# Decoder kernel on one core: passes written out without barriers, two steps of the attentions reordered, and more idle products on TensorE

## Reference

```
x = x + gated causal self-attention(layernorm(x))      # 16 heads of 16
x = x + rotary cross-attention(layernorm(x), ctx)      # 16 heads
x = x + quantised conv feed-forward(layernorm(x))      # 256 -> 1024 -> 256
x = x + self-attention(layernorm(x))                   # 16 heads, not causal
x = x + one-head cross-attention(layernorm(x), ctx)    # 256 wide
x = x + mixture of experts(layernorm(x))               # top 2 of 16, and a shared one
```

## Time and profile before

| | us |
|---|---|
| median of 3 runs | 3564.23 |
| the profiled execution | 3568.19 |
| its span, first to last instruction (46466 instructions) | 3566.9 |
| start of the four passes (first L1955) | 52.87, 930.92, 1816.92, 2691.84 |
| busy: PE, DVE, ACT, GpSimd | 3231.5 (91%), 2350.4 (66%), 1795.1 (50%), 546.5 (15%) |

### The profile page before, as it was taken

How to read it: one execution, slowest core, us unless ns; L and a number is a source line. 1 busy time by engine, 2 the same in 40 slices (tenths; PEclk the granted TensorE clock), 3 DMA queues, 4 the chain that set the end, 5 groups by cost and what they waited for, 6 DMA issues and landing times. The chain is left out here.

```text
span 3566.9 us, 46466 instructions
## 1 busy us (share of the span) xinstructions
PE 3231.5 (91%) x17428; PEld 1735.4 (49%) x17428; DVE 2350.4 (66%) x4375; ACT 1795.1 (50%) x2562; POOL 546.5 (15%) x990
## 2 busy tenths in 40 slices
PE   5998889999899878999999988899998998799999
PEld 3544432368644433236864444323786444432477
DVE  5864578746585557865668556785666744788566
ACT  2454636653346454665344545466434454546643
POOL 0111010014111101002411110100240111010033
PEclk8898979999989897999998989899999898889999
DMA  3222011113021201201302120110231201011023
GB/s 130 39 38 40 1 28 28 19 49 115 30 46 34 37 1 28 37 10 58 112 25 55 25 37 1 36 28 22 68 101 38 39 16 37 1 36 37 23 69 101
DMA packets 119358, 149.14 MB, mean 42 GB/s; under 512 B 25445, under 2 KB 77159, under 8 KB 118835
## 3 DMA queue, kind: packets, MB, share of 16 engines
q1 hardware_dynamic: 119115, 145.95, 17.0%
HBM read 75.46 MB, written 4.46 MB: 22 GB/s over the span
## 5 line engine op out<-in xcount | busy, mean ns | idle before, releaser
L736 DVE TENSOR_REDUCE small<-psum 128x1 f32<-128x512 f32 (+6 forms) x1856 | 1149.1, 659 | 320.2 <-PE psum L607 282.2
L702 ACT ACTIVATE work<-psum 128x1024 f32<-128x1024 f32 (+5 forms) x1024 | 922.1, 935 | 512.4 <-PE psum L634 256.3
L607 PE MATMUL psum<-work 96*128 96x512 bf16 (+4 forms) x2688 | 720.2, 338 | 94.9 <-DVE xn L754 32.6
L1760 PE MATMUL psum<-rounded_work 128*128 128x512 f32 x2592 | 595.9, 391 | 9.9 <-DVE rounded_work L1846 6.5
L630 PE MATMUL psum<-work 99*128 99x512 bf16 (+4 forms) x2048 | 588.5, 371 | 8.8 <-DMA work<-work 7.1
L607 PEld LDWEIGHTS psum<-work 96*128 96x128 bf16 x2688 | 244.2, 103 | 643.8 <-DVE small L736 362.9
L662 PE MATMUL psum<-work 128*32 128x512 f32 (+4 forms) x4480 | 542.9, 537 | 1.6 <-ACT work L702 1.4
L1760 PEld LDWEIGHTS psum<-rounded_work 128*128 128x128 f32 x2592 | 485.6, 188 | 114.2 <-DVE rounded_work L1846 8.3
L630 PEld LDWEIGHTS psum<-work 99*128 99x128 bf16 (+1 forms) x2048 | 183.1, 99 | 208.4 <-ACT work L702 55.8
L1861 ACT CAST rounded_work<-work 128x512 fp32r<-128x512 f32 x144 | 89.6, 622 | 338.9 <-DVE work L1902 317.4
L768 POOL CAST small<-small 128x16 bf16<-128x16 f32 x96 | 19.0, 198 | 1364.3 <-issue 977.7
(11 more groups left out here) (288 smaller groups left out, 3862.8 us busy)
## 6 DMA issues: line engine op xcount, KB each, us to landing
work<-work SPq DMA_DIRECT2D x320, 192.0 KB, 4.3
work<-combine SPq DMA_DIRECT2D x64, 512.0 KB, 4.0
work<-in_w_gate SPq DMA_DIRECT2D x64, 128.0 KB, 3.5
work<-in_w_up SPq DMA_DIRECT2D x64, 128.0 KB, 3.4
work<-in_w_down SPq DMA_DIRECT2D x64, 128.0 KB, 3.7
work<-in_x SPq DMA_DIRECT2D x10, 512.0 KB, 4.8
out<-x SPq DMA_DIRECT2D x8, 512.0 KB, 2.9
work<-work SPq DMA_DIRECT2D x64, 28.9 KB, 2.0
```

The lines of the kernel that those rows point to most:

```text
L607: ins = nc.tensor.matmul(dst[:, c * n:(c + 1) * n], A.q_pair[0:ROWS, slot, h, P * i:P * (i + 1)], A.k_of(pair, h)[0:ROWS, s0:s0 + n], star ...
L702: nc.scalar.activation(probs[0:size, n % 4, :, 0:P * many], banks(2 * (n % 2), 2)[0:size, :, 0:P * many], ACT.Exp, scale=DH ** -0.5).then_ ...
L736: nc.vector.tensor_reduce(tops[:, pair % 2, places[0]:places[-1] + 1:step], src, AX.X, ALU.max) \
L1760: ins = nc.tensor.matmul(dst, a_parts[i], b_parts[j], start=start and n == 0, stop=stop and n == 2, skip_group_check=True)
```

## The change

The loop becomes four copies of the pass in the program, with semaphore counts that run on (`trip` is part of a mark's key, `at_before` is a mark of the pass before). The barriers between passes go; single waits take their place. In the last pass the work for a next pass is left out. In the plan, GpSimd's share of `top` becomes a piece `cut` right behind `join`, the last `top` moves three entries back, and `norm` moves up to stand right behind `spin`. Six places of TensorE get more products that nobody reads.

```diff
+LAST_TOP_LAG = 3
@@ Marks
-        self.values[(name, *key)] = self.count[name]
+        self.values[(self.trip, name, *key)] = self.count[name]
+    def at_before(self, name, *key):
+        return self.sem(name), self.values.get((self.trip - 1, name, *key), 1)
@@ attention_plan
                 if pair and (u, h) == (0, 0):
-                    firsts[-1].append(("join", pair - 1))
-    firsts[-1] += [("join", PAIRS_OF_HEADS - 1), ("top", PAIRS_OF_HEADS - 1)]
+                    firsts[-1] += [("join", pair - 1), ("cut", pair - 1)]
+    firsts[-1] += [("join", PAIRS_OF_HEADS - 1), ("cut", PAIRS_OF_HEADS - 1)]
...
             after(2, "spin", pair)
-            after(3, "norm", pair)
+            after(2, "norm", pair)
...
         plan += entry
+        if gone == len(firsts):
+            entries += 1
+            if entries == LAST_TOP_LAG:
+                plan.append(("top", PAIRS_OF_HEADS - 1))
@@ heads_gpsimd
-                if kind == "top":
+                if kind == "cut":
@@ gated_tensor
-                x_tile("in", i, 0)
+                if m.trip and i % 2 == 0:
+                    pe.wait_ge(*at_before("out_ready", i + 1))
@@ feed_tensor
+            busy_tensor(14)
             pe.wait_ge(*at("numbers_scaled"))
             busy_tensor(7)
...
                     ins.then_inc(*up("rows_spread", i // 4))
+            busy_tensor(6, 0)
             for mm in range(NH):
...
+                if mm == 0:
+                    busy_tensor(6, 0)
-            busy_tensor(14)
+            busy_tensor(22)
             for j in range(NT // 2):
                 turn_tensor("feed", j)
+                if j == 1:
+                    busy_tensor(8)
@@ expert_sync, expert_tensor, expert_scalar, expert_vector
+        more = lambda: m.trip + 1 < B
-            load_next((b + 1) % B, "next")
+            if b + 1 < B:
+                load_next(b + 1, "next")
-            sp.wait_ge(*at("context_loaded", "next"))
-            for j in range(NT // 2):
+            for j in range(NT // 2) if more() else ():
@@ tensor_program
-        def tensor_program():
+        def tensor_program(b):
+            if b:
+                pe.wait_ge(*at_before("context_loaded", "next"))
+                pe.wait_ge(*at_before("turned", "next", 3))
             turn_context()
             gated_tensor()
+            pe.wait_ge(*at("values_copied", 5))
+            busy_tensor(12, value_banks[5])
             heads_tensor(own_heads, gated_banks_free)
...
             cross_tensor(1)
+            pe.wait_ge(*at("cross_rotated", 0))
+            busy_tensor(26, cross_banks[0])
             heads_tensor(cross_heads, cross_banks_free)
@@ gpsimd_program, sync_program
-            pool.wait_ge(out_stored, OUT_STORED)
+            if b:
+                pool.wait_ge(out_stored, OUT_STORED * b)
+                pool.wait_ge(*at_before("x_loaded", "next"))
+                pool.wait_ge(*at_before("second_x_loaded", "next"))
-            sp.wait_ge(*at("filled", "own"))
-            nc.sync.sem_clear(range(out_stored.num, out_stored.num + 1))
@@ the loop
-        with nc.Fori(0, B) as b:
-            tensor_program()
...
-            restart(nc, m, queues)
-        sp.wait_ge(out_stored, OUT_STORED)
+        for b in range(B):
+            m.trip = b
+            tensor_program(b)
...
+        sp.wait_ge(out_stored, OUT_STORED * B)
```

More of the change, by code:

```diff
@@ L54, in __init__ @@
         self.nc, self.ctx, self.values = nc, ctx, values
-        self.sems, self.count = {}, {}
+        self.sems, self.count, self.trip = {}, {}, None
     def sem(self, name):
@@ L63, in up @@
         self.count[name] = self.count.get(name, 0) + by
-        self.values[(name, *key)] = self.count[name]
+        self.values[(self.trip, name, *key)] = self.count[name]
         return self.sem(name), by
     def at(self, name, *key):
-        return self.sem(name), self.values.get((name, *key), 1)
+        return self.sem(name), self.values.get((self.trip, name, *key), 1)
+    def at_before(self, name, *key):
+        return self.sem(name), self.values.get((self.trip - 1, name, *key), 1)
 class Queue:
@@ L202, in attention_plan @@
     per_main = len([x for x in main if x and x[0][0] in ("score", "value")]) / PAIRS_OF_HEADS
-    plan, gone = [], 0
+    plan, gone, entries = [], 0, 0
     for k, entry in enumerate(main):
@@ L220, in build_program @@
         m = Marks(nc, ctx, known)
-        up, at = m.up, m.at
+        up, at, at_before = m.up, m.at, m.at_before
         sb = lambda name, *shape, dtype=F32: ctx.enter_context(nc.sbuf_tensor(name, [P, *shape], dtype))
@@ L263, in load_next @@
             for i0 in (0, NT // 2):
-                nc.sync.dma_start(x_next[:, i0:i0 + NT // 2, :], io["x"][bass.ds(b, 1), P * i0:P * (i0 + NT // 2), :].rearrange("b (i p) d -> p (b i) d", p=P)) \
+                nc.sync.dma_start(x_next[:, i0:i0 + NT // 2, :], io["x"][b:b + 1, P * i0:P * (i0 + NT // 2), :].rearrange("b (i p) d -> p (b i) d", p=P)) \
                     .then_inc(*up(X_LOADED[i0 != 0], tag, by=16))
             for i, n in enumerate(CTX):
-                nc.sync.dma_start(ctx_rows[0:n, i:i + 1, :], io["ctx"][bass.ds(b, 1), P * i:P * i + n, :].rearrange("b p d -> p b d")) \
+                nc.sync.dma_start(ctx_rows[0:n, i:i + 1, :], io["ctx"][b:b + 1, P * i:P * i + n, :].rearrange("b p d -> p b d")) \
                     .then_inc(*up("context_loaded", tag, by=16))
@@ L297, in setup_sync @@
             sp.wait_ge(*at("context_loaded", "first"))
-            nc.sync.sem_inc(out_stored, OUT_STORED)
         OUT_STORED = 2 * 16
@@ L1725, in expert_sync @@
                 sp.wait_ge(*at("out_ready", i1 - 1))
-                nc.sync.dma_start(io["out"][bass.ds(b, 1), P * i0:P * i1, :].rearrange("b (i p) d -> p (b i) d", p=P),
+                nc.sync.dma_start(io["out"][b:b + 1, P * i0:P * i1, :].rearrange("b (i p) d -> p (b i) d", p=P),
                                   x[:, i0:i1, :]).then_inc(out_stored, OUT_STORED // 2)
-            sp.wait_ge(*at("context_loaded", "next"))
         def expert_gpsimd():
@@ L1864, in expert_scalar @@
                     nc.scalar.activation(pr[:, 1, :], pr[:, 0, :], ACT.Exp).then_inc(*up("best_exp"))
-                if u == NEXT_UNIT + 3:
+                if u == NEXT_UNIT + 3 and more():
                     root_scalar("next", 0, NT)
@@ L1925, in expert_vector @@
                 unit(u)
-                step = u - NEXT_UNIT
+                step = u - NEXT_UNIT if more() else -1
                 if 0 <= step < 4:
@@ L2008, in vector_program, with gpsimd_program @@
             expert_vector()
-        def gpsimd_program():
-            pool.wait_ge(out_stored, OUT_STORED)
+        def gpsimd_program(b):
+            if b:
+                pool.wait_ge(out_stored, OUT_STORED * b)
+                pool.wait_ge(*at_before("x_loaded", "next"))
+                pool.wait_ge(*at_before("second_x_loaded", "next"))
             out_gpsimd(own_heads, resident["out0_b"][:, :], x_next)
@@ L2036, in build_program @@
         restart(nc, m, queues)
-        with nc.Fori(0, B) as b:
-            tensor_program()
+        for b in range(B):
+            m.trip = b
+            tensor_program(b)
             scalar_program()
             vector_program()
-            gpsimd_program()
+            gpsimd_program(b)
             sync_program(b)
-            restart(nc, m, queues)
-        sp.wait_ge(out_stored, OUT_STORED)
+        sp.wait_ge(out_stored, OUT_STORED * B)
 def restart(nc, m, queues):
```

## The result

The changed kernel takes 3462.51 us (median of 4 runs, 3460.25 to 3468.0), 0.9708 of the kernel before (95% interval 0.9685 to 0.9731). A second set of five runs beside experiments 6 to 8 gave 3463.16 us and 0.9701 (0.9682 to 0.9720). The forecast was 3467. The sum is right within 5 us; its terms are not all right, and that is what the experiments are about.

A forecast was written before the change was run, and what follows sets the result against it. PE bounds the kernel (busy 91% of the span), through its waits and its time at low clock. Gains 28.5 + 31 + 24 + 13 + 0 + 0.5 = 97 us gave a 3467 us median; 8 in 10: 3441 to 3502.

The forecast's parts named there:

- 19 and 9.5: Pass starts: 19 us from PE's three stops at the barriers, 9.5 from the half clock behind them.
- 28.5: Pass starts: total gain in us from removing the barriers, stops and half clock together; bounds 19 to 29.1.
- 31 forecast: Second attention: `norm` directly behind `spin` removes 24 PE waits for xn, 31 us; bounds 20 to 32.6.
- 24 forecast: All attentions: moving the last `top` removes twelve long PE waits for GpSimd's cuts, 24 us; bounds 15 to 25.6.
- I take 13: Behind eight of the last `top` waits: half clock no longer falls, 13 us gained; bounds 3 and 18.6.
- that rival: Waits move: last pair's rows land late, DVE bounds second attention, clock falls as before; 3501 us, chance 0.13.
- The sum, 0: All added unread products together: gains and losses sum to +1 us, taken as 0.
- so they take about 5.1 us: Own attention's start: the 12 unread products run at low clock and end late, a loss of 5 us; bounds 0 and 7.
- The cross-attention's 0: Ahead of the cross-attention: 26 unread products fit the gap without delay, worth 0; bounds -14 and +18 us.
- `second_tensor`'s 6: Before `second_tensor`: unread products fill gaps so later products and transposes run less at half clock, 6 us; bounds -3 and 9.
- the first rival: Attention starts: clock stays up through them, thanks to the filled waits; 3425 us, chance 0.13.
- Slower by late code: Whole kernel: four copies must stream their code where a loop stood, PE waits for it; 3638 us, chance 0.02.

The follow-up runs named there:

- experiment 6: Changed kernel plus, in the second attention, one unread 128x512 product behind each block of scores ahead of the first exponentials: 3451.49 us, 0.9667.
- experiment 7: Changed kernel plus one unread product behind each such block in all three attentions, eight more ahead of the cross-attention's first transposed scores: 3432.68 us, 0.9617.
- experiment 8: Changed kernel with the router's 32 products in two halves, six wide expert products between them, none added: 3453.72 us, 0.9677.
- experiment 9: Changed kernel without the 12 unread products ahead of the own attention: 3473.79 us, 0.9729.
- experiment 5: The changed kernel itself, run and profiled again without an edit: 3463.16 us, 0.9701.
- experiment 2: Changed kernel with the unread products as in the kernel before, new ones taken out of seven places: 3470.52 us, 0.9725.

## Why the prediction was right, and where it was not

**The barriers.** The mechanism is as written: no stop, no fall of the clock, cover of 4 us left on GpSimd. Of the terms, 19 and 9.5 are found in place (19.3 of stops; the three stages behind them 73.12 to 69.30, 72.18 to 69.31 and 71.64 to 69.30 us, 9.0 in all). The step that failed is "28.5" as a gain of the whole kernel: alone it gave 20, and the clock then fell in other places. How much of the 6.4 us of a stop was the branch and how much the barriers, no run separates. The forecast had treated each stretch at half clock as belonging to the wait ahead of it.

**`norm`.** Right in mechanism, place and size: 31 forecast, 30 measured, pair 23.72 us.

**The last `top`.** The wait was right (24 forecast, 25.5 found). "I take 13" of clock behind it was too small: 16 us in the attentions and 13 more in stages further on, 54.8 in the profiles and 57 by the ratios. The rows landed in time, so that rival had nothing.

**Products nobody reads.** The sum, 0, was near the 7 measured, but by two errors. For the own attention the failed step is "so they take about 5.1 us": it took the moment of the fall from the trace of before. Timelines of PE in the changed kernel, first and second pass:

```profile
118.05 4.11 PE L964 MATMUL psum<-ident,work 128*128 128x8 f32 x32
122.00 5.28 PE L1338 MATMUL psum<-ident_bf 128*128 128x512 bf16 x12
127.08 0.63 PE L615 MATMUL psum<-work 96*128 96x128 bf16 x4
```

```profile
972.32 3.63 PE L964 MATMUL psum<-ident,work 128*128 128x8 f32 x32
975.81 2.75 PE L1338 MATMUL psum<-ident_bf 128*128 128x512 bf16 x12
979.82 0.40 PE L615 MATMUL psum<-work 96*128 96x128 bf16 x4 [1.26 <-DVE gate L1166]
```

In the first pass it is as forecast: 5.28 us at the low clock, no wait left and a late start. In the other three the stage had begun at the full clock, L964 was over by 975.81, and the products took 2.75 us at the full clock inside a wait of 4.0; in experiment 9, with that wait empty, the clock fell in it. That the barriers' edit made this term a gain is argued from the two timelines; no run has the products with the barriers. The cross-attention's 0 was right. `second_tensor`'s 6 was too much: the stage is 4.0 us shorter than before (2.3 in experiment 5), and 2.4 (0.7) shorter than without the products. The last pass's 0.5 was not tried alone.

**The sum.** The parts' single effects are 20, 30, 57 and 7, together 114 us; the whole gave 105 (0.0295 x 3566). They overlap: an edit that keeps the clock up in one place is worth more or less according to where the others let it fall. That the forecast came within 5 us is in part luck. The top's 20 us and the products' 7 above their terms stand against 8.5 too much for the barriers and 9 of overlap, which the sum left out. One step of the ranges is off too: halfway between 3467 and the first rival's 3425 is 3446, not 3441; the result lies inside either.

**Rivals.** Slower by late code did not come: 141 pieces arrive instead of 146, and no wait for "issue" at the pass starts. The first rival, clock up through the attentions' starts, was half right. The own attention has 40.3 us at half clock (52.4 in experiment 5) instead of 85.5. The products are a part of that, since without them it has 63.0 (experiment 2). In the cross and second attention the clock fell as the forecast said: ahead of the fall in the second attention each block is 0.39 us of PE's work in DVE's 0.60. Experiments 6 and 7 show that this rival's mechanism is real if the products stand between the blocks. The clock then stays at 1.0 where only filling the wait ahead had not kept it. The Trainium skill's page "TensorE: Matmul & The Clock Gate" (A second HAM failure mode: psum-queue depth-cycling) describes such short idle spells between groups of products that cycle through banks, and a clock that goes up and down with them. The trace agrees in the fall; but here the clock then stayed at 0.50 for the whole stretch, with PE busy for 16.98 of 17.10 us. The price in the second attention was the 8.1 us of experiment 6, for 99.3 us of PE busy at half clock.

## What to carry to other kernels

Products that nobody reads belong where another engine sets TensorE's pace, one between each two blocks and short enough for that pace, more than in front of such a stretch. Halving a stretch at low clock is worth only what the next engine leaves: read DVE's busy share in the same window first. And a gain from the clock is not a property of one edit: sum the whole kernel's time at either level before and after, and measure parts both alone and taken out, because every edit moves the moments at which the clock falls. Profile the same kernel twice before a few microseconds of one stage are read as an effect.

## What was not expected of the hardware

The clock fell while TensorE was busy without a gap, behind a row of narrow products. In the changed kernel the 32 router products of 16 columns take 3.64 us and the stretch from them on has a mean of 0.76; with six wide products in their middle it is 1.00 (experiment 8). PE was busy for all of both windows. And whether a fall comes depends on the moment as well. The same instructions had 3.4 us at half clock in the kernel before (in one pass of four), 13.7 with only the passes changed, 20.5 and 23.9 in two executions of the changed kernel, and 27.3 without the 12 products. And half clock can be free: in the second attention the blocks that run ahead, 17.4 us of them, began at the same times at 0.50 as at 1.00 (experiment 6).
